# VectorE's and the head's order of work in a fused kernel of a state-space block, an MLP and an FP4 feed-forward

## What is computed

```python
def fp4_quant_dequant(x):          # blocks of 16 along the last axis
    scale = maximum(max(abs(xb)) / 6.0, 1e-12)
    return GRID[searchsorted(MID, abs(xb / scale))] * sign(xb) * scale

def fp4_linear(x, w):
    return einsum('bsk,nk->bsn', fp4_quant_dequant(x), fp4_quant_dequant(w))

def ffn(x):                        # w_gate, w_up: 1408 x 512, w_down: 512 x 1408
    h = silu(fp4_linear(x, w_gate)) * fp4_linear(x, w_up)
    return fp4_linear(h, w_down)

def attn(x):                       # scan: 16 states a channel
    x = x + ssm_scan(rmsnorm(x, scale1), A, B, C, D)
    h = rmsnorm(x, scale2)
    return x + gelu(h @ w1 + b1) @ w2 + b2

xn = layernorm(x)
result = x + attn(xn) + ffn(xn)
```

## Time and profile before

| | |
|---|---|
| time, median of 3 runs | 3159.74 us (3159.46 to 3160.57) |
| the profiled execution: time, span | 3159.74 us, 3157.9 us |
| TensorE busy | 3067.0 us, 97% of the span |
| VectorE busy | 2046.9 us, 65% |
| ScalarE busy | 1088.4 us, 34% |
| GpSimd busy | 1146.3 us, 36% |

### The profile page before, as it was taken

The page is one execution under the profiler, slowest core; times in us unless marked ns, Lnnn a source line. Parts: engine busy times, 40 slices in busy tenths (PEclk is TensorE's granted clock), DMA queues, the critical chain, the costliest instruction groups (busy, mean ns, idle before and its releaser), DMA issues.

```text
span 3157.9 us, 43122 instructions
## 1 busy us (share of the span) xinstructions
PE 3067.0 (97%) x14861; PEld 2472.7 (78%) x14861; DVE 2046.9 (65%) x4427; ACT 1088.4 (34%) x1910; POOL 1146.3 (36%) x1097
## 2 busy tenths in 40 slices
PE   5899999999999999999999999999999999999999
PEld 3678888888877777777777788888888888888887
DVE  8798898987777766767777754444445444454442
ACT  5445655645444333333422321212122121121211
POOL 7556656655555544545554210110011111111000
PEclk9999999999999999999999999999999999999999
DMA  4133434357766656666643533333333333333320
GB/s 123 45 92 86 119 112 122 92 138 184 186 176 166 162 152 170 158 157 171 163 99 94 127 72 71 73 73 71 78 67 79 74 68 71 71 73 74 71 60 14
DMA packets 865577, 335.58 MB, mean 106 GB/s; under 512 B 680400, under 2 KB 771792, under 8 KB 862800
## 3 DMA queue, kind: packets, MB, share of 16 engines
q1 hardware_dynamic: 865360, 332.83, 43.1%
HBM read 225.21 MB, written 107.51 MB: 105 GB/s over the span
## 4 chain that ended last, share of the span: by engine, by line
PE 69%; DVE 15%; issue 5%; POOL 4%; DMA 3%; SPq 2%; ACT 2%; DVEq 0%; POOLq 0%; ACTq 0%
PE bank L875 22%; PE bank L891 22%; PE bank L752 14%; PE bank L774 7%; DVE qs L995 3%; POOL qa L1541 2%; DVE qa L1012 2%; PE bank L815 2%; DVE qs L1006 1%; DVE qa L968 1%; DVE qb L1020 1%; POOL qa L1535 1%; PE bank L823 1%; SPq L493 1%; PE bank L722 1%
## 5 line engine op out<-in xcount | busy, mean ns | idle before, releaser
L875 PE MATMUL bank<-hT,Wp 128*128 128x512 f32 x3072 | 744.9, 391 | 2.4 <-DVE Wp L1182 2.4
L891 PE MATMUL bank<-Wp,G 128*128 128x512 f32 x3072 | 744.0, 391 | 0.0
L875 PEld LDWEIGHTS bank<-hT,Wp 128*128 128x128 f32 x3072 | 577.3, 188 | 128.1 <-issue 2.8
L891 PEld LDWEIGHTS bank<-Wp,G 128*128 128x128 f32 x3072 | 576.9, 188 | 126.3
L752 PE MATMUL bank<-XT,Wg 128*128 128x512 f32 (+1 forms) x2148 | 526.8, 394 | 10.6 <-DVE Wd L1027 5.4
L752 PE MATMUL bank<-XT,Wu 128*128 128x512 f32 (+1 forms) x2148 | 514.1, 388 | 15.9 <-DVE sg L960 15.6
L774 PE MATMUL bank<-Wd,HT 128*128 128x512 f32 x2112 | 515.6, 393 | 6.8 <-POOL HT L1549 6.3
L1231 DVE CAST G<-gf 128x512 fp32r<-128x512 f32 x256 | 110.8, 433 | 608.9 <-PE bank L891 589.8
L752 PEld LDWEIGHTS bank<-XT,Wu 128*128 128x128 f32 x2148 | 400.1, 189 | 106.3 <-issue 25.7
L752 PEld LDWEIGHTS bank<-XT,Wg 128*128 128x128 f32 x2148 | 400.1, 191 | 100.7 <-issue 12.3
L774 PEld LDWEIGHTS bank<-Wd,HT 128*128 128x128 f32 x2112 | 391.7, 188 | 106.0 <-issue 14.3
(11 more groups left out here) (114 smaller groups left out, 2829.5 us busy)
## 6 DMA issues: line engine op xcount, KB each, us to landing
px<-in_L_attn_x_dram SPq DMA_DIRECT2D x128, 256.0 KB, 3.3
xin<-in_L_attn_x_dram SPq DMA_DIRECT2D x128, 256.0 KB, 3.6
sT<-r_K SPq DMA_DIRECT2D x128, 256.0 KB, 4.1
r_Z<-xin SPq DMA_DIRECT2D x64, 256.0 KB, 2.4
r_U<-ub SPq DMA_DIRECT2D x16, 1024.0 KB, 6.7
sU<-r_U SPq DMA_DIRECT2D x32, 512.0 KB, 5.3
r_Y<-sY SPq DMA_DIRECT2D x16, 1024.0 KB, 5.6
xl<-in_L_attn_x_dram SPq DMA_DIRECT2D x64, 256.0 KB, 3.1
```

The lines of the kernel that those rows point to most:

```text
L875: ins = e.matmul(bk[:], Wp[f][wh][:, 0, k * P:(k + 1) * P], hT[xh][b % 2][:, k, :], start=(k == 0 and p_ == 0), stop=(k == KD - 1 and p_ = ...
L891: ins = e.matmul(ACC[j][:], G2[gh][:, n % 2, j * P:(j + 1) * P], Wp[f][wh][:, 1, :], start=(f == 0 and p_ == 0), stop=(f == 15 and p_ == 2))
```

## The change

Work is moved within the engines' programs; no arithmetic changes.

- TensorE: `gu_half(1, 0)`, which was issued in four pieces behind `minus_high(28)` to `minus_high(31)` in the head, is issued in window 1.
- VectorE: `h_mult(s)` stood ahead of `h_back(s - 1)` in window `s`; it now stands at the start of window `s + 1`, behind `h_back(s - 1)` and a late `x_turn`. `h_mult(0)` leaves the head with it (it stood at `m` = 31).
- VectorE: parts 1 and 2 of `prepare` stand ahead of `mid_a` of the side job and the h job, where they stood behind `mid_b`; part 0 moves the other way, from there to the end of the window, behind `h_back` and ahead of `w_low`.
- ScalarE: the copy that makes `nI`, with its wait for the constants, stands ahead of the head's loop instead of at `m` = 3, and `silu(0)` behind the loop instead of at `m` = 28.

```diff
--- before.py
+++ after.py
@@ -829,8 +829,7 @@
             def window(s):
                 k = s - S0
                 if s < NW:
-                    if s > SW:
-                        gu_half(s, 0)
+                    gu_half(s, 0)
                     gu_half(s, 1)
                 if side(s - 2) in TPOS:
                     turn(side(s - 2))
@@ -900,8 +899,6 @@
                 minus_high(m)
                 if 18 <= m < 26:
                     gu_half(0, (m - 18) // 4, range((m - 18) % 4, (m - 18) % 4 + 1))
-                elif 28 <= m < 32:
-                    gu_half(1, 0, range(m - 28, m - 27))
             for s in range(SW, NW + 1):
                 window(s)
                 if s >= PRE0 and (s - PRE0) // 3 < 4 and (s - PRE0) % 3 == 2:
@@ -1128,6 +1125,7 @@
                 h, x_ = h_job(s), side(s)
                 fronted, low_x = side(s - 1), side(s - 3)
                 outputs = 0 <= k < 2 * NV and k % 2
+                h_mult(s - 1)
                 if low_x in TPOS:
                     low(low_x)
                 elif low_x is not None and prompt(low_x):
@@ -1149,8 +1147,10 @@
                 for step in todo[0:6 if s < 14 else 3]:
                     step()
                 del todo[0:6 if s < 14 else 3]
-                if PRE0 <= s < PRE0 + 12 and (s - PRE0) % 3 == 0:
-                    prepare((s - PRE0) // 3, 0)
+                if PRE0 <= s < PRE0 + 12 and (s - PRE0) % 3 == 1:
+                    prepare((s - PRE0) // 3, 1)
+                if PRE0 + 3 <= s < PRE0 + 15 and (s - PRE0) % 3 == 0:
+                    prepare((s - PRE0) // 3 - 1, 2)
                 if outputs:
                     ssm_scan(k // 2, 1)
                 if fronted is not None:
@@ -1164,12 +1164,6 @@
                     if SIDE[s][0] == "x":
                         x_norm(x_, place(x_), lambda: e.wait_ge(d_xs[place(x_)], 16 * loads(x_)))
                     front(x_)
-                if PRE0 <= s < PRE0 + 12 and (s - PRE0) % 3 == 1:
-                    prepare((s - PRE0) // 3, 1)
-                if PRE0 + 3 <= s < PRE0 + 15 and (s - PRE0) % 3 == 0:
-                    prepare((s - PRE0) // 3 - 1, 2)
-                if s < NW:
-                    h_mult(s)
                 h_back(s - 1)
                 if low_x in XPOS and not prompt(low_x):
                     x_turn(low_x)
@@ -1255,8 +1249,6 @@
                     inverse(m)
                 if m >= 2:
                     mid_b(m - 2)
-                if m == 31:
-                    h_mult(0)
                 if m < 2:
                     stats(2 * m)
                     stats(2 * m + 1)
@@ -1267,6 +1259,8 @@
                 del steps[0:2]
             for s in range(SW, NW + 1):
                 window(s)
+                if PRE0 <= s < PRE0 + 12 and (s - PRE0) % 3 == 0:
+                    prepare((s - PRE0) // 3, 0)
                 if 0 <= s - (NW - 3) < 4:
                     w_low(s - (NW - 3))
             gelu_parts(0)
@@ -1484,20 +1478,18 @@
                     e.wait_ge(s_glo, n - 1)
                 e.activation(gf[:, n % 2], PB[n % 2][:], ACT.Gelu, bias=vec[:, f:f + 1]).then_inc(s_gl, 1)
 
+            e.wait_ge(d_cs, 16)
+            e.activation(nI[:], ident, ACT.Copy, scale=-1.0).then_inc(s_ni, 1)
             for m in range(NJ + 4):
-                if m == 3:
-                    e.wait_ge(d_cs, 16)
-                    e.activation(nI[:], ident, ACT.Copy, scale=-1.0).then_inc(s_ni, 1)
                 if m >= 4:
                     high(m - 4)
-                if m == 28:
-                    silu(0)
                 if m < NJ:
                     weight_inverse(m)
                 if 1 <= m <= NJ:
                     magnitude(m - 1)
                 if m >= 4:
                     low(m - 4)
+            silu(SW - 1)
             for s in range(SW, NW + 1):
                 window(s)
                 if s >= PRE0 and (s - PRE0) // 3 < 4:
```

## The result

The changed kernel takes 3181.62 us (median of 4 runs, 3181.39 to 3182.23), the kernel before 3159.97: 21.7 us more. All 13 of its executions on record, the profiled one among them, lie between 3181.39 and 3189.15 with a mean of 3184.3, 24.3 us more; that is the ratio of 1.0077, with the 95% interval 1.0063 to 1.0089. Measured again, beside some of the experiments, it took 26.6 us more, 1.0082 (1.0068 to 1.0095). The forecast was +0.6 and a range up to 3172; the change is slower, and outside of it.

The account below looks back on a forecast made before the run. It took TensorE as bound, with gains only from its waits (11.2 + 9.4 + 4.8 us) and the opening. Terms 3.1 + 2.5 + 2.0 - 2.0 - 5.0 = +0.6 gave 3160.3 us, range 3152 to 3172.

Parts of the forecast that it names:

- The landing and the head: Head: `nI` waiting for the constants' transfer costs +3.1 us; `gu_half(1, 0)` and `silu(0)` behind the head cost +2.5.
- Over eleven windows VectorE's loop changes by +0.3: Windows up to the state-space part: moving `h_mult` lengthens VectorE's loop by 0.3 us per eleven windows; +2.0 taken in all.
- its three cases: Window kinds for moved `h_mult`: no side job 0 us; with `x_turn` +0.6; with side x job -0.5.
- some five groups: Stretch up to the state-space windows: about five groups of eleven windows paced by VectorE, each charged +0.3 us.
- State-space windows, -2.0: State-space windows: VectorE has time, and the five waits for scans, 4.8 us in all, shrink by 2.0 us.
- `prepare`, -5.0: Last windows before the MLP: moving `tile_root`, `tile_low` and `tile_add` shortens TensorE's waits, -5.0 us together.
- The slow one: Rival, chance 0.17: VectorE's loop lengthens in the middle; `x_turn` windows give +16 (3176 us), plain windows too +30 (3190).
- The faster rival: Rival, chance 0.15: waits before the MLP go but 2 us and the constants cost nothing; -6.7, 3153 us.
- The third: Rival, chance 0.10: the `prepare` move gains nothing as `h_mult` stays as late; -5 becomes 0, 3165 us.

Follow-up runs that it names:

- head_only: Kernel before with only the head moves (`nI`, `silu(0)`, `gu_half(1, 0)`, `h_mult(0)`), windows unchanged: +7.2 us, ratio 1.0020.
- constants_only: Kernel before with only the copy that makes `nI` moved ahead of ScalarE's head loop: +5.2 us, ratio 1.0013.
- mult_before_turn: Kernel before with `h_mult` moved directly behind `h_back`, ahead of the late `x_turn`: +25.2 us, ratio 1.0079.
- swap_x: Kernel before with `h_mult` moved behind `h_back` only in windows with a side x job: -5.7 us, ratio 0.9982.
- prepare_only: Kernel before with only the three parts of `prepare` moved: -3.1 us, ratio 0.9991.
- constants_first: Kernel before with `nI` ahead of ScalarE's head loop and the `cs` transfer issued second instead of eighth: +1.0 us, ratio 1.0003.

## Why the prediction was wrong

**The landing and the head: right.** `nI` was made at 9.15 us (9.6 forecast), the second reciprocal ran at 11.23 (11.7):

```profile
9.15 0.31 ACT L1482 ACTIVATE nI<-cs 128x128 fp32r<-128x128 f32 x1 [7.13 <-DMA cs<-in_constants_dram]
9.37 0.21 ACT L1307 ACTIVATE qs<-qs 128x32 f32<-128x32 f32 x1
9.73 1.06 POOL L1527 TENSOR_TENSOR qa<-xin,qs 128x512 f32<-128x512 f32 x1 [5.17 <-ACT qs L1307]
...
11.23 0.35 DVE L997 RECIPROCAL qs<-qs 128x32 f32<-128x32 f32 x1 [3.66 <-POOL qs L1515]
```

```profile
cs<-in_constants_dram SPq DMA_DIRECT2D x1, 74.5 KB, 5.1
```

+2.6 where I had +3.1. The end of the head:

```profile
114.66 0.60 ACT L1311 ACTIVATE XT<-bank 128x512 fp32r<-128x512 f32 x1 [0.88 <-PE bank L733]
115.27 1.28 ACT L1326 ACT_TABLE_LOAD   x1
116.57 0.38 ACT L1326 ACTIVATE sg<-bank 128x256 f32<-128x256 f32 x1
116.98 0.42 DVE L957 TENSOR_TENSOR sg<-bank,sg 128x256 f32<-128x256 f32 x1 [8.27 <-ACT sg L1326]
117.09 2.90 PE L752 MATMUL bank<-XT,Wg 128*128 128x256 f32 x12 [2.48 <-ACT sg L1326]
...
120.72 0.42 DVE L1009 SCALAR_TENSOR_TENSOR qa<-bank,qa 128x256 f32<-128x256 f32 x1 [1.05 <-ACT bank L1291]
```

The last `low` came at 114.66 although all began 2.6 later, so leaving out the matmuls and `silu(0)` saved 2.5 and not 1.6. Then the table load, the activation right behind it and `gu_half(1, 0)`, in the open as forecast, but 2.90 us and not 2.26; why it was slower no run shows. `mid_a` of the first h job at 120.72, 5.0 later against 5.6. +4.7 at window 2, +5.5 at window 4, forecast +5.6.

**`h_mult(s)` behind `h_back(s - 1)`: the step that failed.** It is the term "Over eleven windows VectorE's loop changes by +0.3", taken as +2.0 for the whole stretch; the stretch cost 18.8 us, and 17.4 with the swap alone. The mechanism had been named and put among the rivals (0.17); its three cases were mis-sized, all in one direction. All three had been worked out from one window, which itself has an `x_turn` (at 826.06). A window with `x_turn` costs 0.80, not 0.6; a plain window 0.29, not 0; a window with a side x job gives back 0.28, not 0.5. By eleven windows that is 4 x 0.80 + 3 x 0.29 - 4 x 0.28 = +2.95. The difference has one known part: I took a wait for the instruction right ahead to be free. `h_mult` and `h_rows` as neighbours cost 0.2 us (measured in the windows with `x_turn`, 4.81 against 4.60). In the other two cases, where they are neighbours too, the same 0.2 takes the forecast to +0.2 and -0.3. In the windows with a side x job the exchange saves 0.52 on the `tensor_scalar` and pays that 0.2.

The second fault is in the count: the gain or loss of a loop that VectorE paces was entered for "some five groups". The windows from 14 to 99 are 7.7 groups. At +0.3 a group that alone would have made 2.3 us; at +2.95 it makes 22.8. That TensorE waited for `h_mult` only 13 times said that VectorE was never far behind, not that it had room: any lengthening of its loop had to come out as TensorE's waits.

**State-space windows, -2.0: wrong.** The stage cost +3.8. The waits for scans fell by more than forecast (4.8 to 0.4), but the waits for `h_mult` rose from 3.2 us in 2 pieces before to 8.6 in 5, and two of the five, at 1191.66 and 1237.06, are 2.93 long. The timeline at both:

```profile
1188.50 0.55 DVE L978 TENSOR_SCALAR qa<-xin,mv,rst 128x512 f32<-128x512 f32 x1 [6.11 <-DMA xin<-in_L_attn_x_dram]
...
1190.28 0.65 DVE L971 STREAM_TRANSPOSE qb<-qa 128x512 f32<-128x512 f32 x1
...
1190.86 0.65 DVE L957 TENSOR_TENSOR sg<-bank,sg 128x512 f32<-128x512 f32 x1
...
1191.66 4.58 PE L752 MATMUL bank<-XT,Wu 128*128 128x512 f32 x12 [2.93 <-DVE sg L957]
...
1237.06 4.38 PE L752 MATMUL bank<-XT,Wu 128*128 128x512 f32 x12 [2.93 <-DVE sg L957]
```

The same row of the kernel before, in the first of these windows:

```profile
1162.61 3.01 PE L752 MATMUL bank<-XT,Wu 128*128 128x512 f32 x12 [1.57 <-DVE sg L960]
```

VectorE had waited 6.11 us for the tile of the side x job, 5.39 before. What stood behind `x_norm` came late: `h_mult` before, `h_back` (0.65) and then `h_mult` now. Of the 1.36 us by which TensorE's wait is longer, 0.7 are the transfer's, which also varies where the order is the old one (5.34 to 6.43 us in head_only and constants_only), and 0.6 the swap's. I had looked at what the swap gives the scans, and not at what else hangs on `h_mult` behind a late transfer.

The second part is the clock. TensorE had idled 2.93 us, and the clock that it was granted then fell from 2.4 to 1.2 GHz for a while (0.72 of full on the mean from 1191 to 1197 and from 1236 to 1242; 1.00 in the same windows before). The twelve matmuls took 4.58 and 4.38 us instead of 3.01 and 3.00, 2.9 us for both. Waits +5.4, clock +2.9, scans -4.4 make +3.9. No experiment separates the clock from the wait ahead of it. In the other profiles with the whole swap the stage is at +0.9, +0.6, +0.5 and, in mult_before_turn, +3.1.

**`prepare`, -5.0: right alone, and spent by the swap.** Alone it gives -4.4. The same windows are nearly all plain ones, in which the late `h_mult` costs 5.5 (1.7 of it clock). My sum put these windows to `prepare` only and left the swap's own price out of them.

**The rivals.** The slow one came true in its first form: +16 from the windows with `x_turn` (18.1 found), and in its second half too (14 for the plain windows, 7.1 found), set off by the side x windows (-7.8). Of its two answers, 3176 and 3190, the result lies between. Its evidence against, "the stall ends with GpSimd's instruction to within 0.05 us", was true, and did not bear: the stall was swallowed, but more than the stall had been added. The faster rival did not come: neither did the constants come for nothing nor did the waits before the MLP go. The third did not either: moved alone, `prepare` does what it says (-4.4).

## What to carry to other kernels

Before an instruction is moved on an engine that sets the pace, ask which idle time it fills where it stands. `h_mult` filled half of VectorE's wait for another engine, for nothing; behind that wait it cost its full length and opened the gap. The same move paid in the windows in which other work had already bridged the wait, so set the order by kind of window and not once for all.

Measure the stretch that a swap touches from end to end in one window of each kind, and multiply by the number of windows; 0.26 us a window on the mean, 85 times, came to more than all that was moved at the head and the tail.

## What the runs showed of the hardware

`h_rows` (a transposition) right behind `h_mult`, whose output it needs: it starts 0.10 us behind the other's end and takes 0.71 instead of 0.67; with `x_turn` in between it starts 0.07 before that one's end. The price is not the same for every such pair: the `tensor_scalar` at 852.91 starts 0.03 behind the end of the `tensor_reduce` that it needs. The Trainium skill, "VectorE: DVE Perf Modes", section "The DRAIN you can't avoid", has it that a semaphore between two operations costs nothing extra (eight copies took the same time with and without). No run here has the same pair with and without its semaphore. What the traces show is that a wait on the instruction right ahead is not free: an independent one in between saves 0.2 us (4.60 against 4.81).

VectorE's `tensor_scalar` on 128 x 32 values took 0.72 us where it started 0.60 behind GpSimd's `h_low`, and ended 0.03 behind it. In the window after, `h_low` was nearly over when it started at 828.08, and it took 0.18:

```profile
826.88 1.30 POOL L1549 TENSOR_TENSOR HT<-qb,HT 128x512 fp32r<-128x512 f32 x1 [1.49 <-ACT HT L1325]
```

In none of the 85 windows before did it end ahead of the `h_low` that it met. Nearly all that swap_x gains comes from that 0.5 us.

The landing of one and the same transfer was 2.5 us behind one other, 5.1 to 5.6 behind seven.

TensorE's granted clock fell from 2.4 to 1.2 GHz for a while behind some of its waits and not behind others: behind 1.81 us idle at 1162.13 in prepare_only (0.72 on the mean from 1162 to 1168), but not behind 2.49 at 1208.14 in constants_first (1.00 from 1208 to 1214). Where it fell, twelve matmuls of 128x512 took 4.4 to 5.5 us instead of 2.9 to 3.0. So a profile can hold some microseconds of it in one stage (4.0 in swap_x), and another profile none.
